# Four-layer graph network, attention layer: sums inverted one unit later, and a unit's transposes issued ahead of the next score products

## The reference

```python
h = jnp.maximum(_layernorm(x, axis=-1), 0.0)
q, k, v = (proj(Wq, bq), proj(Wk, bk), proj(Wv, bv))        # 8 heads of 32
scores = jnp.einsum('bhqd,bhkd->bhqk', q, k) * SCALE
scores = scores * (adj_matrix + bond_matrix)[:, None, :, :]  # both are adj
attn = jax.nn.softmax(scores, axis=-1)
ctx = jnp.einsum('bhqk,bhkd->bhqd', attn, v)
x = x + jnp.einsum('bse,fe->bsf', ctx, Wo) + bo
```

## Time and profile before

| | us |
|---|---|
| median of three runs | 2968.77 |
| the profiled execution, its own time | 2966.04 |
| its span, first to last instruction | 2962.9 |
| TensorE (PE) busy | 2841.6 (96%) |
| VectorE (DVE) busy | 1856.5 (63%) |
| ScalarE (ACT) busy | 1486.9 (50%) |
| GpSimd (POOL) busy | 721.2 (24%) |

### The profile page before, as it was taken

The page is one execution under the profiler, slowest core; times in us unless marked ns, Lnnn a source line. Parts: engine busy times, 40 slices in busy tenths (PEclk is TensorE's granted clock), DMA queues, the critical chain, the costliest instruction groups (busy, mean ns, idle before and its releaser), DMA issues.

```text
span 2962.9 us, 62026 instructions
## 1 busy us (share of the span) xinstructions
PE 2841.6 (96%) x21888; PEld 2255.5 (76%) x21888; DVE 1856.5 (63%) x4010; ACT 1486.9 (50%) x2761; POOL 721.2 (24%) x1305
## 2 busy tenths in 40 slices
PE   8999999999999999999999999999999999999999
PEld 6777787787877878778687786877868778687786
DVE  3787427874288742887428864388643886438862
ACT  2883318833288232873228732387323873238622
POOL 0342003420034201342013420134101441014410
PEclk9999999999999999999999999999999999999999
DMA  5552215522165131651316513155122551226500
GB/s 176 186 165 93 90 61 191 162 91 107 50 201 168 69 129 39 201 178 49 136 45 197 181 50 122 63 189 180 63 101 77 189 181 65 82 81 197 169 8 15
DMA packets 198987, 355.12 MB, mean 120 GB/s; under 512 B 22033, under 2 KB 126865, under 8 KB 198673
## 3 DMA queue, kind: packets, MB, share of 16 engines
q1 hardware_dynamic: 197136, 346.81, 35.1%
q0 software_dynamic: 1536, 4.20, 0.4%
HBM read 212.25 MB, written 84.15 MB: 100 GB/s over the span
## 4 chain that ended last, share of the span: by engine, by line
PE 70%; DVE 15%; issue 8%; ACT 3%; SPq 2%; DMA 1%; DVEq 1%; POOL 0%; ACTq 0%; POOLq 0%
PE ps L1265 37%; PE ps L1488 7%; PE ps L1431 7%; PE ps L1551 7%; PE ps L1453 6%; PE ps L1626 4%; DVE junk L974 3%; SPq L508 2%; DVE Z L930 2%; DVE stats L748 1%; DVE h L990 1%; DVE dn L983 1%; DVE h L1008 1%; PE ps L1305 1%; DVE shiftB L1005 1%
## 5 line engine op out<-in xcount | busy, mean ns | idle before, releaser
L1431 PE MATMUL ps<-kS,qS 128*128 128x512 f32 x1024 | 381.4, 455 | 77.8 <-DVE nm L930 74.4
L930 DVE CUSTOM_DVE_ANT_0 Z<-ps,adjN 128x1024 f32<-128x1024 f32 x328 | 394.6, 1208 | 39.4 <-PE ps L1431 35.5
L1188 ACT ACTIVATE Z<-Z,nm 128x1024 f32<-128x1024 f32 x328 | 378.3, 1157 | 18.4 <-POOL nm L685 18.4
L697 POOL TENSOR_SCALAR H<-adjN 128x128 fp32r<-128x128 f32 (+1 forms) x456 | 317.8, 697 | 0.0
L1431 PEld LDWEIGHTS ps<-kS,qS 128*128 128x128 f32 x1024 | 160.6, 189 | 164.8 <-DVE nm L930 124.3
L1178 ACT ACTIVATE PTa<-ps 128x512 f32<-128x512 f32 x448 | 246.6, 599 | 75.2 <-PE ps L1453 62.6
L1453 PE MATMUL ps<-ident,Z 128*128 128x128 f32 x1920 | 253.2, 274 | 6.0 <-ACT Z L1188 4.3
L1453 PEld LDWEIGHTS ps<-ident,Z 128*128 128x128 f32 x1920 | 219.3, 140 | 49.7 <-issue 19.6
L685 POOL TENSOR_TENSOR nm<-nm,minus 128x1 f32<-128x1 f32 x512 | 98.2, 192 | 571.7 <-DVE nm L930 570.7
L930 DVE CUSTOM_DVE_ANT_0 Zx<-ps,adjN 128x1024 f32<-128x1024 f32 x184 | 221.3, 1205 | 8.8 <-PE ps L1431 6.9
L1265 PE MATMUL ps<-mh,adjT 128*128 128x256 f32 x1024 | 223.6, 379 | 0.8 <-issue 0.8
(11 more groups left out here) (192 smaller groups left out, 6215.4 us busy)
## 6 DMA issues: line engine op xcount, KB each, us to landing
blocks_kept<-blocks_in SPq DMA_DIRECT2D x144, 512.0 KB, 3.0
blocks_even<-blocks_kept SPq DMA_DIRECT2D x288, 128.0 KB, 3.4
adjT<-adjT_in SPq DMA_DIRECT2D x8, 4096.0 KB, 13.4
adjN<-adj_in SPq DMA_DIRECT2D x8, 4096.0 KB, 15.6
PTb<-blocks_kept SPq DMA_DIRECT2D x192, 128.0 KB, 3.5
adjT<-adjT_in SPq DMA_DIRECT2D x8, 2048.0 KB, 9.1
qS<-qhi SPq DMA_DIRECT2D x112, 128.0 KB, 2.1
qS<-qlo SPq DMA_DIRECT2D x112, 128.0 KB, 2.1
```

Source lines behind the costliest of these rows:

```text
L697: done = pool.tensor_scalar(H[:, t, of], adjN[:, t, of], 0.0, 0.0, ALU.is_equal, ALU.is_equal)
L930: dve.tensor_tensor_reduce(Z_of(u), ps[:, 2 * (u % 2):2 * (u % 2) + 2].rearrange("p a n -> p (a n)"), adjN[:, u // HEADS], SCORE_SCALE, LO ...
L1188: act.activation(Z_of(u), Z_of(u), ACT.Exp, bias=nm[:, u:u + 1], accum_out=sm[:, HEADS * (u // HEADS) + place(u):HEADS * (u // HEADS) + pl ...
L1431: mm = pe.matmul(ps[:, 2 * (u % 2) + s], qS[:, hd, rows(t)], kS[:, hd, half(s)], start=True, stop=True)
```

## The change

Two edits. The step at which VectorE inverts a tile's sums, and with it GpSimd's spreading, goes from 8t+8 to 8t+9; so does TensorE's transposing of the spread inverses. And in every step but the first TensorE's queue has the transposes of unit u-1 ahead of the score products of unit u+2, where they stood behind them. The function that names the waits of the rotating banks (`turns`) counts uses in an order that neither edit alters.

```diff
-        INVERT, SPREAD, COPY, WEIGH, NORMALISE, PROJECT, ADD = 4, 4, 7, 7, 9, 10, 11
+        INVERT, SPREAD, COPY, WEIGH, NORMALISE, PROJECT, ADD = 5, 5, 7, 7, 9, 10, 11
...
                     if u == 0:
                         transposes(0)
+                    if u and (n := turned_at(u)) is not None:
+                        transposes(n)
                     if u + 2 < UNITS:
                         scores(u + 2)
-                    if u and (n := turned_at(u)) is not None:
-                        transposes(n)
                     for part in range(len(PARTS)):
                         if (g := weigh_at.get(u - part)) is not None:
                             weighted_values(g, part)
```

## The result

| | us |
|---|---|
| median before, runs of the same chip | 2968.77 (2966.88 to 2970.8, 5 runs) |
| median after | 2983.82 (2982.61 to 2986.43, 5 runs) |
| ratio after to before, 95% interval | 1.0052 [1.004, 1.0064] |
| the profiled execution after, its own time | 2983.5 |
| its span | 2980.5 |

A forecast was written before the change was run, and what follows sets the result against it. The prediction took a middle tile to be bound by a chain through TensorE's, ScalarE's and VectorE's queues. Terms of 2.4 - 0.2 + 0.2 - 1.15 = +1.25 us a batch, 10.0 in eight, gave 2958.8 us, range 2938 to 2972.

The forecast's parts named there:

- four periods of the middle tiles: Middle tiles of the attention: each period falls by 0.60 us, four of them gain 2.4 us a batch.
- first and second tile, with unit 20: Start of a batch: small losses and gains in the first two tiles and at unit 20, together -0.2 us.
- last tile: Last tile of a batch: the spread inverses leave TensorE 0.14 us sooner ahead of weighted values, a gain of 0.2 us.
- end, by the queue: End of a batch's attention: the spreading stands behind GpSimd's 3.65 us comparison, so 1.15 us a batch is lost.
- end, by the clock: End of a batch's attention: the prediction had no term for a fall of TensorE's clock.
- The rest of the tile: Middle tile from unit 8t+10's multiplication to the end of the next tile's unit 8t+5: stays with VectorE at 7.25 us.
- the first half of the forecast's argument: VectorE in a middle tile: with the reciprocal a unit later, its wait of 1.15 to 1.16 us goes.
- Unit 14: Second tile: transposes ahead of its scores delay its multiplication from 487.22 to 487.84, 0.6 us lost.
- the shorter wait and the pitch give 0.6 back: Second tile: the shorter wait at its reciprocal and the pitch return the 0.6 us lost at unit 14.
- rival C: Score products held up behind transposes become the limit; middle tile stays at 15.8 us, kernel slower at 2978; chance 0.13.
- C's point of decision: Gain of a middle tile, 1.15 / 4 = 0.29 us, below which the kernel is slower.
- The rule: VectorE's gap at the reciprocal: taken by itself the rule makes all 75.4 us the gain, 2893 us; chance 0.02.

The follow-up runs named there:

- e1: Kernel before with only the transposes put ahead of the score products, inversion and spreading at their old steps: 2964.44 us against 2968.61.
- e10: Kernel before with inversion and spreading a unit later except the last tile's, transposes ahead only at places 6 and 0 from the second tile: 2946.61 us against 2969.46.
- e2: Kernel before with only the inversion and spreading a unit later, transposes still behind the score products: 2980.82 us against 2968.61.
- e9: e3 with two unused products of 512 columns on TensorE, filling its wait for the last tile's spreading: 2978.86 us against 2969.46 for the kernel before.
- e3: Kernel before with only the last tile's inversion and spreading a step later: 2983.36 us against 2968.61.
- e4: Kernel after, both edits, but with the last tile's inversion and spreading at the old step: 2967.79 us against 2968.61 for the kernel before.
- e12: Kernel before with inversion and spreading a unit later except in the last tile, transposes behind scores everywhere: 2962.51 us against 2969.46.
- e11: Kernel before with transposes ahead only at places 6 and 0 from the second tile on, inversion and spreading at old steps: 2949.77 us against 2969.46.
- e5: Kernel after with GpSimd's 3.65 us comparison of the whole last tile moved behind the last tile's spreading: 2966.3 us against 2969.22 for the kernel before.
- e6: e3 with four unused products of 512 columns on TensorE during its wait for the last tile's spreading: 2988.62 us against 2969.22 for the kernel before.

## Why the prediction was wrong

**The steps that failed.** Gains of a batch by the terms of the forecast's sum, from the table of stretches above:

| gain of a batch, us | forecast | measured |
|---|---|---|
| four periods of the middle tiles (M26 to M58) | +2.40 | +1.14 |
| first and second tile, with unit 20 (M0 to M26) | -0.20 | -0.66 |
| last tile | +0.20 | -0.26 |
| end, by the queue | -1.15 | -1.18 |
| end, by the clock | nothing | -0.73 |
| sum | +1.25 | -1.69 |

The middle tiles' gain was taken at twice its size, the second tile was to give back what it doesn't, and the fall of the clock isn't in the sum at all. With the measured middle tiles and every other term as forecast the sum would have been nothing.

**The middle tiles: right mechanism, half the size.** The wait of the reciprocal went, the gap moved to the score products, and the starts on TensorE came within 0.03 us of the forecast. The period fell by 0.31, not 0.60. Three terms make the difference. From scores to the multiplication that awaits them it took 0.99 (523.20 to 524.19), not the 0.90 that I had from the earlier trace rows: 0.1. The rest of the tile, which I gave to VectorE at its old 7.25, took 7.44 (527.74 to 535.18): unit 8t+12 comes 1.35 behind 8t+11 instead of 1.21, because the spread inverses behind the weighted values take 0.27 and transposes follow them before its scores (529.73, 530.00, 530.80): 0.14. Another 0.05 is spread over the tile. Four periods gave 1.23 in seven batches and 0.57 in the eighth, 1.14 as a mean, instead of 2.4. e1 has the same period without the later inversion: the order alone takes the reciprocal's wait away, and moving the reciprocal, the first half of the forecast's argument, gives nothing on top of it.

**First and second tile: wrong, and by something I didn't look for.** Forecast -0.2 a batch; measured 0.61 lost to M18. Unit 14 itself came 0.75 late (2.21 behind unit 13 instead of 1.46), where I worked out 0.6. What failed was the sentence that the shorter wait and the pitch give 0.6 back: units 17 and 18 give back 0.08. That sentence treats the transposes as ready once their exponential is, and forgets the bank, which waits for VectorE's addition. It is rival C's mechanism, a score product held up behind a waiting transpose, but with another releaser than I named. Places 6 and 0 alone (e10) leave it out and have M10 to M18 at 14.86. Unit 20 came 0.53 late, of which 0.45 is a wait for its scores, where I said 0.3. M18 to M26 also holds a fifth gap of the kind that the four periods have, which the sum left out; its gain and unit 20's loss leave 0.05 lost.

**The last tile:** +0.2 forecast, -0.26 measured, 2 us in eight batches. It is the order's: e1 has it (12.68) and e2 hardly (12.48).

**The end of the batch: the queue's 1.15 was right, and was not all.** The path through GpSimd, `Rs`, `hh`, `hl` and `ctxn` cost 1.18 (e9). What I left out is what the longer idle time does to TensorE's clock: another 5.8 us in the profiled execution, four falls of 1.46 or so. My own bounds for the end, 0.85 to 2.2, hold the sum of 1.91; the value I took didn't.

**The sum.** Eight batches of -1.69 are 13.5 us; with the 1.4 of the start and the 2.7 between the layers this is the 17.6 us of span. By medians, e3's part is 14.8 and e4's -0.8, together 14.0 of the 15.05 measured. Rival C's 2978 was nearest, by a middle tile that gives almost nothing; that is luck, for the measured middle tile gives its 0.31, just above C's point of decision of 0.29, and the second tile and the clock decide instead.

**The rule.** The Trainium skill, Perfetto Trace Analysis, section Optimization Strategy, would have one find the gap of the most contended engine and start what blocks it sooner. Taken as the gain, the gap was 75.4 us; e12 removes the reciprocal's wait in every tile but the last, 61.9 of these, and is 6.95 us faster, since 1.07 of a middle tile's 1.15 reappears at two instructions close by. e11 is nearer to what the rule asks for: the reciprocal stays where it was and the transposes that hold up its exponential start sooner. It gained 19.7 us, still far from the gap. The rule names a place to look, and here not its price.

## What to carry to other kernels

Where several engines are nearly full, as here, a wait that is taken away can come back a few instructions later (1.07 of 1.15 us did); follow the chain back past the releaser until it closes on itself (here copies, transposes of two units earlier, scores in front of them), and change the order only at the places that lie on it: two places of eight gained 0.7%, all eight gained 0.1%. Before moving a step in one queue, list what each other queue has between the old and the new place; a 0.86 us instruction that slipped behind one of 3.65 us cost 14.8 us in eight batches, and swapping these two repaired it. Ask of each stretch in which TensorE will now stand idle what the clock did behind such stretches; a term for it was missing here. When a transpose or product is moved ahead, its output bank must be free as well as its input ready: ask who empties it, and what stands in front of that.

## What the runs showed of the hardware

Behind an idle stretch of TensorE of 1.97 to 2.02 us at the end of the attention the granted clock fell to 0.50 (the 1.2 GHz level) for about 3.4 us, but not each time: in 4 of 8 batches of the kernel after, 6 of 8 of e2 and 3 of 8 of e3, with the same instructions and waits in every batch. What decides which batch falls stays open. With the idle time at 0.7 or 0.83 (before, e5) or filled by products (e6, e9) it happened in none of 8. One fall cost 1.42 to 1.49 us. At the start of an execution, between 15 and 23 us into it, the profiled executions of nine of the twelve experiments and of the kernel after had a fall too, of 3.4 or of 6.8 us, and the first multiplication came 1.1 to 1.5 us later than in the kernel before with the short one and 2.2 to 2.6 with the long one. The kernel before, e1, e4 and e5 had none. That is not tied to any edit here and stays open.
